# Seven half-size products for eight in a two-tile linear layer (one level of Strassen's algorithm)

## The chip, the cores and the metric

One core of one Trainium2 chip. The metric is the device time of one execution in microseconds (us). PE is TensorE's matmul stream, PEld its weight loads, DVE VectorE, ACT ScalarE, POOL GpSimd, SP the engine whose queue issues the DMAs.

## What is computed

```python
def _L0_cond_ref(x, weights, condition):
    W = weights[condition]
    return jnp.einsum('bct,bcd->bdt', x, W)

def _L0_ffn_ref(x, W, b, A, B, p_scores):
    C_CLAMP, EPS = 0.5, 1e-06
    z = jnp.einsum('bsd,od->bso', x, W) + b
    u = jnp.einsum('bsd,edr->ebsr', x, A)
    m = jnp.einsum('ebsr,ero,e->bso', u, B, p_scores)
    norm_z = jnp.linalg.norm(z, axis=-1, keepdims=True)
    norm_m = jnp.linalg.norm(m, axis=-1, keepdims=True)
    gamma = jnp.minimum(C_CLAMP * norm_z / (norm_m + EPS), 1.0)
    return z + gamma * m

x = x + _L0_ffn_ref(_L0_cond_ref(x, cond_weights, itok), W, b, A, B, p_scores)
```

x is 128 x 64 x 1024 in fp32, W is 1024 x 1024, the pair A, B has 8 x 16 = 128 inner columns, and each of the 128 batches picks one of 16 mixing matrices of 64 x 64.

## The kernel before

A tile is two batches: 128 rows of 1024. There are 64 tiles; four make a loop body (`step`, written out once before and once after the loop for the ends). For each tile PE does four things.

- `mix` (L419): eight fp32 matmuls give y transposed, in two halves of four chunks each, into `mix_ps`. ACT casts a half to `y_hi` (L245) and DVE makes the rest, `y_lo` (L333); both are fp32r, a form of fp32 that PE takes in one pass, and three matmuls (hi·hi, hi·lo, lo·hi) stand for one product.
- `linear` (L439): z in two halves of 512 columns, each 8 chunks x 3 passes = 24 matmuls with 512 columns.
- `down` (L430), once per two tiles: u, 24 matmuls of 256 columns. `up` (L456): m, six matmuls of 512 columns.

DVE adds the bias to each half (`add_bias`, L368), ACT squares and sums it (L289) and m (L313), POOL adds the residual to half 0 (L224) and takes the roots (L227, L232), DVE adds it to half 1, makes gamma (L388 to L401) and adds gamma·m (L408). SP loads x and stores the result. The mixers are copied by ACT from a table in SBUF (L253). Each engine has its own list of instructions; what orders them between engines are semaphores, written out by hand. In the head, ACT and DVE split W chunk by chunk (`split_w`, L241, L327), and the first tile's z takes each chunk as it comes:

```python
pe.wait_ge(w_hi_ready, k + 1)
pe.wait_ge(w_lo_ready, k + 1)
for h in range(2):
    summed = linear_chunk(0, h, k)
```

## Time and profile before

| | |
|---|---|
| three runs | 1031.59, 1031.59, 1031.82 us |
| profiled execution: span from first to last instruction | 1029.6 us |
| what lies around the span | about 2.0 us (run time less span) |
| instructions | 15207, of them 5260 matmul records |
| busy: PE, DVE, ACT, POOL | 1017.3, 351.2, 289.2, 165.2 us |
| mean granted clock of TensorE | 0.997 |
| moved by DMA | 73.58 MB |

Busy time is the time in which an engine had an instruction in it; matmuls are pipelined and overlap, so a group's sum can be above the span. The page also has the chain that ended last, the groups of instructions by line with what ended the idle time before them, and the DMA queues.

### The profile page before, as it was taken

How to read it: one execution, taken by the hardware profiler on the slowest of the kernel's cores; microseconds unless marked ns; L12 is line 12 of the kernel's file. 1: busy time of each engine (PE TensorE's matmuls, PEld its weight loads, DVE VectorE, ACT ScalarE, POOL GpSimd, SP SyncE). 2: the span in 40 equal slices, each digit the busy share in tenths (PEclk: the TensorE clock that was granted, in tenths of full speed). 3: DMA queues.
4: the chain of work that ended last, by engine and by line, in shares of the span. 5: the costliest groups of instructions: out<-in, count | busy, mean ns of one | idle time of the engine just before them, and what ended most of it. 6: DMA issues, size and time to landing. Idle time of an engine off the chain costs nothing.

```text
span 1029.6 us, 15207 instructions
## 1 busy us (share of the span) xinstructions
PE 1017.3 (99%) x5260; PEld 856.4 (83%) x5260; DVE 351.2 (34%) x620; ACT 289.2 (28%) x685; POOL 165.2 (16%) x263
## 2 busy tenths in 40 slices
...
PEclk9999999999999999999999999999999999999999
...
DMA packets 21367, 73.58 MB, mean 71 GB/s; under 512 B 2409, under 2 KB 3434, under 8 KB 21354
## 3 DMA queue, kind: packets, MB, share of 16 engines
...
q14 instruction: 5, 0.04, 0.0%
...
## 4 chain that ended last, share of the span: by engine, by line
PE 98%; DMA 1%; DVE 0%; ACT 0%; SPq 0%; issue 0%; DVEq 0%; POOLq 0%; POOL 0%; ACTq 0%
PE z_ps L439 70%; PE mix_ps L419 11%; PE m_ps L456 9%; PE u_ps L430 9%; DMA x_in<-in_x_dram 1%; DVE w_lo L327 0%; SPq L172 0%; ACT w_hi L241 0%; DVE rows L408 0%; DVE rows L368 0%; DVEq L59 0%; ACT squares L289 0%; POOLq L59 0%; ACT y_hi L245 0%; SPq L170 0%
## 5 line engine op out<-in xcount | busy, mean ns | idle before, releaser
L439 PE MATMUL z_ps<-w_hi,y_hi 128*128 128x512 f32 x1024 | 415.9, 406 | 2.2 <-DVE w_lo L327 2.2
L439 PE MATMUL z_ps<-w_hi,y_lo 128*128 128x512 f32 x1024 | 405.8, 396 | 0.0
L439 PE MATMUL z_ps<-w_lo,y_hi 128*128 128x512 f32 x1024 | 405.4, 396 | 0.0
L289 ACT ACTIVATE squares<-rows 128x512 bf16<-128x512 f32 x128 | 80.8, 631 | 628.2 <-DVE rows L368 536.8
L439 PEld LDWEIGHTS z_ps<-w_hi,y_lo 128*128 128x128 f32 x1024 | 192.7, 188 | 46.3
L439 PEld LDWEIGHTS z_ps<-w_hi,y_hi 128*128 128x128 f32 x1024 | 193.4, 189 | 43.0 <-ACT y_hi L245 2.4
L439 PEld LDWEIGHTS z_ps<-w_lo,y_hi 128*128 128x128 f32 x1024 | 193.4, 189 | 40.9
L368 DVE TENSOR_TENSOR rows<-z_ps,bias 128x512 f32<-128x512 f32 x128 | 88.6, 692 | 365.7 <-PE z_ps L439 365.7
L333 DVE TENSOR_TENSOR y_lo<-mix_ps,y_hi 128x512 fp32r<-128x512 f32 x128 | 88.2, 689 | 232.7 <-ACT y_hi L245 232.5
L224 POOL TENSOR_TENSOR rows<-rows,x_in 128x512 f32<-128x512 f32 x64 | 81.7, 1277 | 428.0 <-DVE rows L368 428.0
L419 PEld LDWEIGHTS mix_ps<-mixer,x_in 128*128 128x128 f32 x1024 | 131.3, 191 | 10.8 <-DMA x_in<-in_x_dram 2.3
L419 PE MATMUL mix_ps<-mixer,x_in 128*128 128x128 f32 x1024 | 134.6, 275 | 1.7 <-DMA x_in<-in_x_dram 1.7
L408 DVE SCALAR_TENSOR_TENSOR rows<-m_ps,gamma,rows 128x1024 f32<-128x1024 f32 (+1 forms) x65 | 82.3, 1268 | 2.2
L245 ACT CAST y_hi<-mix_ps 128x512 fp32r<-128x512 f32 x128 | 73.3, 572 | 18.3 <-PE mix_ps L419 18.3
L430 PE MATMUL u_ps<-y_hi,a_hi 128*128 128x256 f32 x256 | 71.8, 280 | 0.0
L430 PE MATMUL u_ps<-y_lo,a_hi 128*128 128x256 f32 x256 | 71.6, 280 | 0.0
L430 PE MATMUL u_ps<-y_hi,a_lo 128*128 128x256 f32 x256 | 71.4, 279 | 0.0
L313 ACT ACTIVATE squares<-m_ps 128x1024 bf16<-128x1024 f32 x64 | 65.5, 1023 | 2.3 <-PE m_ps L456 0.5
L229 POOL TENSOR_TENSOR z_sum<-z_sq 128x1 f32<-128x1 f32 x64 | 12.3, 193 | 315.4 <-ACT squares L289 315.4
L227 POOL TENSOR_TENSOR norm_m<-m_sq,half 128x1 f32<-128x1 f32 x64 | 35.1, 548 | 111.0 <-ACT squares L313 111.0
L430 PEld LDWEIGHTS u_ps<-y_lo,a_hi 128*128 128x128 f32 x256 | 48.2, 188 | 1.4
L430 PEld LDWEIGHTS u_ps<-y_hi,a_hi 128*128 128x128 f32 x256 | 48.1, 188 | 1.4
...
## 6 DMA issues: line engine op xcount, KB each, us to landing
x_in<-in_x_dram SPq DMA_DIRECT2D x64, 512.0 KB, 3.3
out_dram<-rows SPq DMA_DIRECT2D x63, 512.0 KB, 2.7
rows<-in_L_ffn_W_dram SPq DMA_DIRECT2D x4, 512.0 KB, 7.4
w_late<-in_L_ffn_W_dram SPq DMA_DIRECT2D x4, 512.0 KB, 11.0
...
a_in<-in_L_ffn_A_dram SPq DMA_DIRECT2D x1, 512.0 KB, 14.3
bm_in<-in_L_ffn_B_dram SPq DMA_DIRECT2D x1, 512.0 KB, 8.9
bias<-in_L_ffn_b_dram SPq DMA_DIRECT2D x1, 512.0 KB, 9.2
```

Source lines behind the costliest of these rows:

```text
L224: nc.gpsimd.tensor_tensor(result[:, j % 2, 0:H], z_b[:, j % 2, 0:H], x_in[:, j, 0:H], ALU.add).then_inc(residual_0_ready, 1)
L227: nc.gpsimd.tensor_tensor(norm_m[:, one], m_sq[:, one], half[:, :], ALU.pow).then_inc(norm_m_ready, 1)
L245: nc.scalar.copy(y_hi[:, j // 2 % 2, h * HC:(h + 1) * HC, j % 2 * P:(j % 2 + 1) * P], mix_ps[h][:, :].rearrange("p (k n) -> p k n", k=HC)) ...
L289: nc.scalar.activation(squares[:, cols], z_b[:, j % 2, cols], ACT.Square, accum_out=z_sq[:, j % 2, h:h + 1]).then_inc(z_squared, 1)
L313: nc.scalar.activation(squares[:, :], m_ps[:, :], ACT.Square, accum_out=m_sq[:, j % 2:j % 2 + 1]).then_inc(m_squared, 1)
L333: nc.vector.tensor_tensor(y_lo[part], mix_ps[h][:, :].rearrange("p (k n) -> p k n", k=HC), y_hi[part].bitcast(fp32), ALU.subtract).then_in ...
L368: nc.vector.tensor_tensor(z_b[:, j % 2, cols], z_ps[h][:, :], bias[:, cols], ALU.add).then_inc(z_b_ready, 1)
L408: nc.vector.scalar_tensor_tensor(out=result[:, j % 2, c], in0=m_ps[:, c], scalar=gamma[:, one], in1=result[:, j % 2, c], op0=ALU.mult, op1 ...
L419: mixed = nc.tensor.matmul(mix_ps[h][:, k * P:(k + 1) * P], x_in[:, j % BODY, (h * HC + k) * P:(h * HC + k + 1) * P], mixer[:, j % 2, :], ...
L430: summed = nc.tensor.matmul(u_ps[:, 0:2 * P], left[:, k, :], right[:, g, k, :], start=(k == 0 and n == 0), stop=(k == KC - 1 and n == 2))
L439: summed = nc.tensor.matmul(z_ps[h][:, :], left[:, g, k, r], right[:, k, h * H:(h + 1) * H], start=(k == 0 and n == 0), stop=(k == KC - 1 ...
L456: summed = nc.tensor.matmul(m_ps[:, c], left[:, r], right[:, c], start=(n == 0), stop=(n == 2))
```

## The change

Two tiles are a pair, and the pair's 256 rows are sorted anew into two row blocks of 128: block r holds 32 of the 64 output channels of each of the pair's four batches (the mixer's columns are laid out so that `mix` writes them in this order, 64 columns of either block per chunk and tile). With the two halves of the 1024 inner columns, Y is 2 x 2 blocks of 128 x 512, and W is 2 x 2 blocks of 512 x 512. In place of eight products come seven, in Winograd's form:

- S3 = Y11 − Y21, S2 = Y22 − S3, S4 = Y12 − S2, S1 = Y21 + Y22 on DVE, for each tile, read from PSUM; `y21` is a copy by ACT. S2 and S3 lie in `s23`, S4 and S1 are written back into `mix_ps`. All four are split into `s_hi` (ACT) and `s_lo` (DVE), as Y11, Y12, Y21, Y22 are into `y_hi`, `y_lo`.
- T1 = W12 − W11, T3 = W22 − W12, T2 = W22 − T1, T4 = W21 − T2 on POOL, once, in the head; the seven matrices W11, W21, W22, T1, T3, T4, T2 lie split in `w_hi`, `w_lo`. W is loaded in four chunks of a megabyte, through the two halves of `z` as staging space.
- P1 = Y11·W11 and P2 = Y12·W21 in bank `a_ps`; P6 = S2·T2, on top of it P7 = S3·T3, and later P4 = Y22·T4 in `b_ps`; P5 = S1·T1 and on top of it P3 = S4·W22 in `c_ps`. Each is 4 chunks x 3 passes = 12 matmuls of 512 columns (`product`).
- z11 = P1 + P2 + b, u2 = P1 + P6, u3 = u2 + P7, z12 = u2 + P5 + P3 + b, z21 = u3 + P4 + b, z22 = u3 + P5 + b: P1 is copied by ACT, the sums with a PSUM bank are DVE's, the bias for z12, z21 and z22 is added by POOL in SBUF.
- The residual is added by POOL for a whole row block (1024 columns), from `x_res`, which holds the x of one row block, loaded a second time in the new order of rows. The mixers are loaded by SP straight from DRAM, two small DMAs a tile, each behind a register load of the batch's id; their zeros are set once. x has two buffers in place of four. m's squares are taken in halves. `up` for pair p−1 stands within pair p, and for the last pair behind it.

```diff
+    W11, W21, W22, T1, T3, T4, T2 = range(7)
...
+w_hi = sb("w_hi", [P, 7, HC, H], fp32r)
+w_lo = sb("w_lo", [P, 7, HC, H], fp32r)
...
+y0_hi = sb("y0_hi", [P, HC, 2 * P], fp32r)
+y0_lo = sb("y0_lo", [P, HC, 2 * P], fp32r)
+y1_hi = sb("y1_hi", [P, 2, HC, 2 * P], fp32r)
+y1_lo = sb("y1_lo", [P, 2, HC, 2 * P], fp32r)
+s_hi = sb("s_hi", [P, 2, HC, 2 * P], fp32r)
+s_lo = sb("s_lo", [P, 2, HC, 2 * P], fp32r)
...
+mix_ps = pb("mix_ps", [P, 2, H])
+a_ps = pb("a_ps", [P, H])
+b_ps = pb("b_ps", [P, H])
+c_ps = pb("c_ps", [P, H])
...
+    for k in range(2, HC):
+        sp.wait_ge(w_lo_ready, 2 * (k - 1))
+        sp.wait_ge(t_lo_ready, 2 * (k - 1))
+        sp.dma_start(z[:, k % 2, :, :], w_steps[k]).then_inc(w_loaded[k], 16)
...
+    for k in range(HC):
+        st = z[:, k % 2, :, :]
+        pool.wait_ge(w_lo_ready, 2 * k + 1)
+        nc.gpsimd.tensor_tensor(st[:, 0, 0:H], st[:, 0, H:D], st[:, 0, 0:H], ALU.subtract).then_inc(t1_made, 1)
+        pool.wait_ge(w_lo_ready, 2 * k + 2)
+        nc.gpsimd.tensor_tensor(st[:, 0, H:D], st[:, 1, H:D], st[:, 0, H:D], ALU.subtract).then_inc(t13_made, 1)
+        pool.wait_ge(t1_made, k + 1)
+        pool.wait_ge(t13_made, k + 1)
+        nc.gpsimd.tensor_tensor(st[:, 1, H:D], st[:, 1, H:D], st[:, 0, 0:H], ALU.subtract).then_inc(t2_made, 1)
+        pool.wait_ge(t2_made, k + 1)
+        nc.gpsimd.tensor_tensor(st[:, 1, 0:H], st[:, 1, 0:H], st[:, 1, H:D], ALU.subtract).then_inc(t24_made, 1)
...
+        for j in range(2):
+            p = 2 * i + j
+            opening = first and j == 0
+            if not opening:
+                residual(p - 1, 1 - j, 0)
+                norm_z(p - 1, 1 - j, 0)
+                norm_m(p - 1, 0)
+                residual(p - 1, 1 - j, 1)
+                norm_z(p - 1, 1 - j, 1)
+            pool.wait_ge(u2_ready, p + 1)
+            nc.gpsimd.tensor_tensor(z[:, j, 0, H:D], z[:, j, 0, H:D], bias[:, H:D], ALU.add).then_inc(u2_biased, 1)
+            pool.wait_ge(u3_ready, p + 1)
+            nc.gpsimd.tensor_tensor(z[:, j, 1, H:D], z[:, j, 1, 0:H], bias[:, H:D], ALU.add).then_inc(u3_biased1, 1)
+            nc.gpsimd.tensor_tensor(z[:, j, 1, 0:H], z[:, j, 1, 0:H], bias[:, 0:H], ALU.add).then_inc(u3_biased0, 1)
+            if not opening:
+                norm_m(p - 1, 1)
...
+            if not opening:
+                split_s(2 * p + 1, 1, None)
+                act.wait_ge(z21_ready, p)
+                square_z(1 - j, 1, 0, 8 * p - 5)
+            act.wait_ge(p_done[1], p + 1)
             if opening:
...
+            nc.scalar.copy(z[:, j, 0, 0:H], a_ps[:, :]).then_inc(p1_ready, 1)
+            if not opening:
+                square_m(p - 1, 0)
+            if not opening:
+                square_m(p - 1, 1)
+            act.wait_ge(u_done, p + 1)
+            nc.scalar.copy(u_hi[:, :], u_ps[:, 0:2 * P]).then_inc(u_hi_ready, 1)
+            act.wait_ge(z22_ready, p + 1)
+            square_z(j, 1, 1, None if opening else 8 * p)
+            if not closing:
+                split_y(2 * p + 2, 0, 1 - j)
+            if not closing:
+                split_s(2 * p + 2, 0, p + 1)
+            act.wait_ge(z12_ready, p + 1)
+            square_z(j, 0, 1, 8 * p + 1)
+            act.wait_ge(z11_ready, p + 1)
+            square_z(j, 0, 0, 8 * p + 2)
+            if not closing:
+                split_y(2 * p + 3, 1, 1 - j)
...
+    def make_s(t):
+
+        dve.wait_ge(s3_made, t + 1)
+        nc.vector.tensor_tensor(s23[:, :, 0, :], block(1, 1), s23[:, :, 1, :], ALU.subtract).then_inc(s2_made, 1)
+        dve.wait_ge(s2_made, t + 1)
+        nc.vector.tensor_tensor(block(1, 0), block(1, 0), s23[:, :, 0, :], ALU.subtract).then_inc(s4_made, 1)
+        nc.vector.tensor_tensor(block(1, 1), block(1, 1), y21[:, :, :], ALU.add).then_inc(s1_made, 1)
+
+    def split_s(t, j):
+
+        for h in range(2):
+            dve.wait_ge(s_hi_ready, 2 * t + h + 1)
+            nc.vector.tensor_tensor(s_part(s_lo, j, h), s23[:, :, :, :] if h == 0 else mixed(1),
+                                    s_part(s_hi, j, h).bitcast(fp32), ALU.subtract).then_inc(s_lo_ready, 1)
...
+    split_y(0, 0, 0, True)
+    make_s(0)
+    split_w(0)
+    split_s(0, 0)
+    split_y(1, 1, 0)
+    split_w(1)
+    make_s(1)
+    split_t(0)
+    split_s(1, 1)
+    split_t(1)
+    for k in range(2, HC):
         split_w(k)
+        split_t(k)
...
+        for j in range(2):
+            p = 2 * i + j
+            opening, closing = first and j == 0, last and j == 1
+            if not opening:
+                make_s(2 * p + 1)
+                finish_z21(p - 1, 1 - j)
+                split_s(2 * p + 1, 1)
+                make_gamma(p - 1, 0)
+            dve.wait_ge(p_done[6], p + 1)
+            dve.wait_ge(p1_ready, p + 1)
+            nc.vector.tensor_tensor(z[:, j, 0, H:D], b_ps[:, :], z[:, j, 0, 0:H], ALU.add).then_inc(u2_ready, 1)
+            if not opening:
+                add_m(p - 1, 1 - j, 0)
+            dve.wait_ge(p_done[7], p + 1)
+            if not first:
+                dve.wait_ge(out_stored[1], 16 * (p - 1))
+            nc.vector.tensor_tensor(z[:, j, 1, 0:H], b_ps[:, :], z[:, j, 0, 0:H], ALU.add).then_inc(u3_ready, 1)
+            dve.wait_ge(p_done[5], p + 1)
+            dve.wait_ge(u3_biased1, p + 1)
+            nc.vector.tensor_tensor(z[:, j, 1, H:D], c_ps[:, :], z[:, j, 1, H:D], ALU.add).then_inc(z22_ready, 1)
+            dve.wait_ge(u_hi_ready, p + 1)
+            nc.vector.tensor_tensor(u_lo[:, :], u_ps[:, 0:2 * P], u_hi[:, :].bitcast(fp32),
+                                    ALU.subtract).then_inc(u_lo_ready, 1)
+            if not closing:
+                split_y(2 * p + 2, 0, 1 - j)
+                make_s(2 * p + 2)
+            dve.wait_ge(p_done[3], p + 1)
+            dve.wait_ge(u2_biased, p + 1)
+            nc.vector.tensor_tensor(z[:, j, 0, H:D], c_ps[:, :], z[:, j, 0, H:D], ALU.add).then_inc(z12_ready, 1)
+            if not closing:
+                split_s(2 * p + 2, 0)
+            if not opening:
+                make_gamma(p - 1, 1)
+                add_m(p - 1, 1 - j, 1)
+            dve.wait_ge(p_done[2], p + 1)
+            nc.vector.tensor_tensor(z[:, j, 0, 0:H], a_ps[:, :], bias[:, 0:H], ALU.add).then_inc(z11_ready, 1)
+            if not closing:
+                split_y(2 * p + 3, 1, 1 - j)
...
+    def product(bank, hi, lo, n, start):
+
+        for k in range(HC):
+            passes = [(hi, w_hi), (hi, w_lo), (lo, w_hi)]
+            for i, (left, right) in enumerate(passes):
+                summed = nc.tensor.matmul(bank[:, :], left[:, k, :], right[:, n, k, :],
+                                          start=(start and k == 0 and i == 0),
+                                          stop=(k == HC - 1 and i == 2), skip_group_check=not start)
...
-    def linear_chunk(j, h, k):
-
-        g, r = j // 2 % 2, slice(j % 2 * P, (j % 2 + 1) * P)
-        passes = [(y_hi, w_hi), (y_hi, w_lo), (y_lo, w_hi)]
-        for n, (left, right) in enumerate(passes):
-            summed = nc.tensor.matmul(z_ps[h][:, :], left[:, g, k, r], right[:, k, h * H:(h + 1) * H],
-                                      start=(k == 0 and n == 0), stop=(k == KC - 1 and n == 2))
-        return summed
-
-    def linear(j, h):
-
-        for k in range(KC):
-            summed = linear_chunk(j, h, k)
-        summed.then_inc(z_done, 1)
...
+            pe.wait_ge(y_lo_ready, 4 * p + 3)
+            if opening:
+                pe.wait_ge(w_hi_ready, 2 * (HC - 1) + 1)
+                pe.wait_ge(w_lo_ready, 2 * (HC - 1) + 1)
+            else:
+                pe.wait_ge(z11_ready, p)
+            product(a_ps, y0_hi[:, :, r0], y0_lo[:, :, r0], W11, True).then_inc(p_done[1], 1)
...
+                    pe.wait_ge(out_ready, 2 * p - 2)
+                up(0)
...
+            if opening:
+                pe.wait_ge(t_hi_ready, 2 * HC)
+                pe.wait_ge(t_lo_ready, 2 * HC)
+            else:
+                pe.wait_ge(z21_ready, p)
+            product(b_ps, s_hi[:, 0, :, r0], s_lo[:, 0, :, r0], T2, True).then_inc(p_done[6], 1)
+
+            pe.wait_ge(s_hi_ready, 4 * p + 4)
+            pe.wait_ge(s_lo_ready, 4 * p + 4)
+            if not opening:
+                pe.wait_ge(z12_ready, p)
+            product(c_ps, s_hi[:, 1, :, r1], s_lo[:, 1, :, r1], T1, True).then_inc(p_done[5], 1)
+
+            pe.wait_ge(u2_ready, p + 1)
+            product(b_ps, s_hi[:, 0, :, r1], s_lo[:, 0, :, r1], T3, False).then_inc(p_done[7], 1)
+
+            if not opening:
+                pe.wait_ge(out_ready, 2 * p - 1)
...
+            down(j)
+
+            if not closing:
+                pe.wait_ge(x_loaded[0], 16 * (p + 2))
+                pe.wait_ge(mixer_loaded[0], 16 * PER * (p + 2))
+                for h in range(2):
+                    mix(0, h)
+
+            pe.wait_ge(z22_ready, p + 1)
+            product(c_ps, s_hi[:, 1, :, r0], s_lo[:, 1, :, r0], W22, False).then_inc(p_done[3], 1)
+
+            pe.wait_ge(p1_ready, p + 1)
+            product(a_ps, y1_hi[:, j, :, r0], y1_lo[:, j, :, r0], W21, False).then_inc(p_done[2], 1)
+
+            if not closing:
+                pe.wait_ge(x_loaded[1], 16 * (p + 2))
+                pe.wait_ge(mixer_loaded[1], 16 * PER * (p + 2))
+                pe.wait_ge(s3_made, 2 * p + 3)
+                mix(1, 0)
+                pe.wait_ge(s_lo_ready, 4 * p + 6)
+                mix(1, 1)
+
+            pe.wait_ge(u3_ready, p + 1)
+            product(b_ps, y1_hi[:, j, :, r1], y1_lo[:, j, :, r1], T4, True).then_inc(p_done[4], 1)
...
     steps(pe, step)
+    pe.wait_ge(u_hi_ready, PAIRS)
+    pe.wait_ge(u_lo_ready, PAIRS)
+    for r in range(2):
+        pe.wait_ge(out_ready, 2 * PAIRS - 2 + r)
+        up(r)
```

**DVE, the middle of a pair.** Before, one tile in the written-out body (line numbers of the kernel before): y_lo for a later tile, the bias sums, gamma, the result.

```order
L333 TENSOR_TENSOR y_lo<-mix_ps,y_hi 128x4x128 [waits y_hi_ready]
L368 TENSOR_TENSOR rows<-z_ps,bias 128x512 [waits z_done]
L333 TENSOR_TENSOR y_lo<-mix_ps,y_hi 128x4x128 [waits y_hi_ready]
L388 TENSOR_SCALAR twice_m<-norm_m 128x1 [waits norm_m_ready]
L391 RECIPROCAL half_over_m<-twice_m 128x1 [waits twice_m_ready]
L368 TENSOR_TENSOR rows<-z_ps,bias 128x512 [waits z_done]
L396 TENSOR_TENSOR rows<-rows,x_in 128x512 [waits z_b_ready]
L401 TENSOR_SCALAR gamma<-norm_z,half_over_m 128x1 [waits over_m_ready,norm_z_ready]
L408 SCALAR_TENSOR_TENSOR rows<-m_ps,gamma,rows 128x1024 [waits residual_1_ready,residual_0_ready,gamma_ready]
```

With the change, from z12 (line numbers of the changed kernel; `s` is `s23`, `stats` holds the small columns): z12, the two s_lo of the next pair's first tile, gamma and the addition of m for block 1 of the pair before, z11, and y_lo, s3, y_lo of the next pair's second tile.

```order
L584 TENSOR_TENSOR z<-c_ps,z 128x512 [waits u2_biased,p3_done]
L504 TENSOR_TENSOR s_lo<-s,s_hi 128x8x64 [waits s_hi_ready]
L504 TENSOR_TENSOR s_lo<-mix_ps,s_hi 128x8x64 [waits s_hi_ready]
L511 TENSOR_SCALAR stats<-stats 128x1 [waits norm_m_ready]
L514 RECIPROCAL stats<-stats 128x1 [waits twice_m_ready]
L517 TENSOR_SCALAR stats<-stats 128x1 [waits over_m_ready,norm_z_ready]
L524 SCALAR_TENSOR_TENSOR z<-m_ps,stats,z 128x1024 [waits residual_ready,gamma_ready]
L591 TENSOR_TENSOR z<-a_ps,bias 128x512 [waits p2_done]
L485 TENSOR_TENSOR y_lo<-mix_ps,y_hi 128x8x64 [waits y21_ready,y_hi_ready]
L490 TENSOR_TENSOR s<-mix_ps,y 128x4x64 [waits s_lo_ready]
L485 TENSOR_TENSOR y_lo<-mix_ps,y_hi 128x8x64 [waits y_hi_ready]
```

The y_lo that the next pair's first product waits for now stands behind the addition of m and z11 on DVE, and z11 in its turn waits for P2.

**POOL, the head.** Before, the three memsets and then the first tile's work:

@@D2B
With the change the four sums of each of the four chunks of T stand there; these are those of chunk 0 and the first of chunk 1:

```order
L290 TENSOR_TENSOR z<-z 128x512 [waits w_lo_ready]
L292 TENSOR_TENSOR z<-z 128x512 [waits w_lo_ready]
L295 TENSOR_TENSOR z<-z 128x512 [waits t13_made,t1_made]
L297 TENSOR_TENSOR z<-z 128x512 [waits t2_made]
L290 TENSOR_TENSOR z<-z 128x512 [waits w_lo_ready]
```

Each waits for DVE's split of W (`w_lo_ready`) or for the sum before it.

**DVE, the head.** With the change, the splits of chunks 2 and 3 of W and T, in this order:

```order
L464 TENSOR_TENSOR w_lo<-z,w_hi 128x512 [waits w_hi_ready]
L467 TENSOR_TENSOR w_lo<-z,w_hi 128x2x512 [waits w_hi_ready]
L473 TENSOR_TENSOR w_lo<-z,w_hi 128x2x512 [waits t_hi_ready]
L476 TENSOR_TENSOR w_lo<-z,w_hi 128x2x512 [waits t_hi_ready]
L464 TENSOR_TENSOR w_lo<-z,w_hi 128x512 [waits w_hi_ready]
L467 TENSOR_TENSOR w_lo<-z,w_hi 128x2x512 [waits w_hi_ready]
L473 TENSOR_TENSOR w_lo<-z,w_hi 128x2x512 [waits t_hi_ready]
L476 TENSOR_TENSOR w_lo<-z,w_hi 128x2x512 [waits t_hi_ready]
```

Chunk 3 of W (L464, L467, the second time) stands behind the split of chunk 2's T, which waits for ACT's casts of what POOL has made.

## Rows read from the trace of the kernel before

**Rows 1.** The page, busy time and the span in 40 slices (PEclk, tenths of full speed):
```profile
PE 1017.3 (99%) x5260; PEld 856.4 (83%) x5260; DVE 351.2 (34%) x620; ACT 289.2 (28%) x685; POOL 165.2 (16%) x263
...
PEclk9999999999999999999999999999999999999999
```

**Rows 2.** The page, the chain that ended last, shares of the span:
```profile
PE z_ps L439 70%; PE mix_ps L419 11%; PE m_ps L456 9%; PE u_ps L430 9%; DMA x_in<-in_x_dram 1%; DVE w_lo L327 0%; SPq L172 0%; ACT w_hi L241 0%; DVE rows L408 0%; DVE rows L368 0%; DVEq L59 0%; ACT squares L289 0%; POOLq L59 0%; ACT y_hi L245 0%; SPq L170 0%
```

**Rows 3.** That chain in order of time (start us, us, what):
```profile
507.88 5.60 PE z_ps L439 x24
...
539.43 5.60 PE z_ps L439 x24
```

**Rows 4.** Timeline of PE (start us, us): first `up` and `down`, and what follows each:
```profile
513.32 0.63 PE L456 MATMUL m_ps<-b_hi,u_hi 128*128 128x512 f32 x2
...
514.72 1.05 PE L419 MATMUL mix_ps<-mixer,x_in 128*128 128x128 f32 x8
...
521.22 0.28 PE L430 MATMUL u_ps<-y_hi,a_hi 128*128 128x256 f32 x1
...
524.02 1.05 PE L419 MATMUL mix_ps<-mixer,x_in 128*128 128x128 f32 x8
```

**Rows 5.** Timeline of the end (start us, us):
```profile
1022.28 0.40 PE L439 MATMUL z_ps<-w_hi,y_lo 128*128 128x512 f32 x1
...
1024.51 0.55 POOL L232 TENSOR_TENSOR norm_z<-z_sum,half 128x1 f32<-128x1 f32 x1
...
1025.34 1.41 DVE L408 SCALAR_TENSOR_TENSOR rows<-m_ps,gamma,rows 128x512 f32<-128x512 f32 x2
1026.12 0.99 SPq L202 DMA_DIRECT2D out_dram<-rows  x2
```

**Rows 6.** The page, DMA issues (count, KB each, median us to landing):
```profile
x_in<-in_x_dram SPq DMA_DIRECT2D x64, 512.0 KB, 3.3
rows<-in_L_ffn_W_dram SPq DMA_DIRECT2D x4, 512.0 KB, 7.4
```

**Rows 7.** Timeline around 500 us, handoffs between engines (start us, us):
```profile
502.97 0.57 ACT L245 CAST y_hi<-mix_ps 128x512 fp32r<-128x512 f32 x1
...
503.57 0.69 DVE L333 TENSOR_TENSOR y_lo<-mix_ps,y_hi 128x512 fp32r<-128x512 f32 x1 [3.57 <-ACT y_hi L245]
...
504.17 0.14 DVE L388 TENSOR_SCALAR twice_m<-norm_m 128x1 f32<-128x1 f32 x1
...
506.60 0.40 PE L439 MATMUL z_ps<-w_hi,y_lo 128*128 128x512 f32 x1
...
507.12 0.69 DVE L368 TENSOR_TENSOR rows<-z_ps,bias 128x512 f32<-128x512 f32 x1 [2.60 <-PE z_ps L439]
```

**Rows 8.** Groups by line (line engine op, count | busy us, mean ns | idle before):
```profile
L368 DVE TENSOR_TENSOR rows<-z_ps,bias 128x512 f32<-128x512 f32 x128 | 88.6, 692 | 365.7 <-PE z_ps L439 365.7
L333 DVE TENSOR_TENSOR y_lo<-mix_ps,y_hi 128x512 fp32r<-128x512 f32 x128 | 88.2, 689 | 232.7 <-ACT y_hi L245 232.5
L224 POOL TENSOR_TENSOR rows<-rows,x_in 128x512 f32<-128x512 f32 x64 | 81.7, 1277 | 428.0 <-DVE rows L368 428.0
L408 DVE SCALAR_TENSOR_TENSOR rows<-m_ps,gamma,rows 128x1024 f32<-128x1024 f32 x63 | 80.9, 1284 | 2.2
L289 ACT ACTIVATE squares<-rows 128x512 bf16<-128x512 f32 x128 | 80.8, 631 | 628.2 <-DVE rows L368 536.8 <-issue 91.4
L245 ACT CAST y_hi<-mix_ps 128x512 fp32r<-128x512 f32 x128 | 73.3, 572 | 18.3 <-PE mix_ps L419 18.3
L377 DVE TENSOR_TENSOR u_lo<-u_ps,u_hi 128x256 fp32r<-128x256 f32 x32 | 13.3, 416 | 1.1 <-ACT u_hi L299 1.1
L327 DVE TENSOR_TENSOR w_lo<-w_late,w_hi 128x1024 fp32r<-128x1024 f32 x4 | 4.9, 1224 | 1.1 <-ACT w_hi L241 1.0
L241 ACT CAST w_hi<-w_late 128x1024 fp32r<-128x1024 f32 x4 | 4.2, 1050 | 1.5 <-DMA w_late<-in_L_ffn_W_dram 1.5
```

**Rows 9.** View of windows, the head (us, PE, PEld, DVE, ACT, POOL busy, PEclk, DMA, GB/s):
```profile
12.50:16.00 3.50, 3.50 (x10) 2.71 (x10) 3.50 (x4) 3.14 (x4) 0.00 (x0) 0.54 1.03 412
```

More of the change, by code:

```diff
@@ L107, in conditioned_clamped_low_rank_linear_kernel @@
-        z_b = rows[:, 0:2, :]
-        result = rows[:, 2:4, :]
-        w_in = [rows[:, k, :] if k < 4 else w_late[:, k - 4, :] for k in range(KC)]
-        mix_ps = [pb(f"mix_ps{h}", [P, H]) for h in range(2)]
-        z_ps = [pb(f"z_ps{h}", [P, H]) for h in range(2)]
+        y21 = sb("y21", [P, HC, C], fp32)
+        s23 = sb("s23", [P, HC, 2, C], fp32)
+        z = sb("z", [P, 2, 2, D], fp32)
+        squares = sb("squares", [P, H], bf16)
+        cond_ids = sb("cond_ids", [1, B], i32)
+        stats = sb("stats", [P, 40], fp32)
@@ new lines, in conditioned_clamped_low_rank_linear_kernel, with z_sq, stat @@
+        half = stats[:, 0:1]
+        p_col = stats[:, 1:2]
+        table_out = stats[:, 2:3]
+        def z_sq(par, r, h):
+            return stats[:, 4 + 4 * par + 2 * r + h:5 + 4 * par + 2 * r + h]
+        def stat(n, r):
+            return stats[:, 12 + 2 * n + r:13 + 2 * n + r]
+        Z_SUM, NORM_Z, M_SQ0, M_SQ1, M_SUM, NORM_M, TWICE_M, HALF_OVER_M, GAMMA = range(9)
+        idle = squares[:, :]
+        a_in = x_res[:, :].rearrange("p (k n) -> p k n", k=KC)
+        bm_in = z[:, 1, 1, :]
```

587 lines of the change are left out of this document (291 added, 296 removed).

## The prediction, made before the changed kernel was run

> **What bounds the kernel now.** The page first: PE is busy 99% of 1029.6 us, at a granted clock of nine tenths or more in every slice [rows 1]. Busy time alone proves little, since matmuls overlap; the chain that ended last does: 98% of it is PE, 70% the z products [rows 2]. So every matmul removed counts in full, as long as the others stay behind PE. The chain in order of time gives the rates. The same piece of 24 z matmuls (one half of one tile) recurs after 31.55 us, which is two tiles, and takes 5.60 us, 0.2333 us a matmul [rows 3]. The 0.40 us in the groups is latency, not rate. In the timeline of PE the six matmuls of `up` take 514.72 − 513.32 = 1.40 us and the 24 of `down` 2.80 us [rows 4]. Two tiles are thus 96 z matmuls (22.40), two `up` (2.80), one `down` (2.80) and, as the rest, 3.55 for the mixes. 32 pairs of tiles are 1009.6 us; 20.0 us of the span are head and tail. From the last matmul's start, 0.23 us before its nominal end, to the end are 7.3 us, so the tail is 7.1 and the head loses 12.9 [rows 5]. The three runs stand at 1031.59 to 1031.82, 2.0 us above the profiled span; I add 2.0 to every span.
>
> **The products.** Seven products of 12 matmuls replace 96 per pair: 12 fewer, in the same shapes (512 columns against a 128x128 weight). Over 32 pairs: 384 x 0.2333 = **−89.6 us**. `up`, `down` and the mixes keep their counts and sizes. A pair is then 28.76 us of PE. SP's queue gets, per pair, four small mixer loads, each behind a register load, and two loads of residual rows into one buffer, on top of its two x loads and two stores. On the scale of the walk below a residual load is asked for at 1.2, when POOL has used the rows before, lands 3.3 us later [rows 6] at about 5 and is wanted at 6.9; the next is asked for at 9.5 and wanted at 26.8. The x and mixer loads asked for at 18.6 and 26.0 are wanted a whole pair later. SP's waits stand in the order in which they are met (1.2, 9.4, 9.4, 18.6, 25.3, 26.0). So they cost nothing; without that cover the first residual load would be 1.9 us of slack gone, on POOL.
>
> **Is PE still covered within a pair?** I walk one pair from the start of P1 (product P1 = 0). PE: P1 to 2.8, `up` 4.2, P6 7.0, P5 9.8, P7 12.6, `up` 14.0, `down` 16.8, mix of the next pair's first tile 18.6, P3 21.4, P2 24.2, mix of its second tile 26.0, P4 28.8. The handoffs: PE to DVE 0.29 us after a product's nominal end (last matmul 506.60 + 0.23, DVE at 507.12), ACT to DVE 0.03, DVE to its next queued operation 0.09 before the first has ended (503.57 + 0.69, next at 504.17) [rows 7]. Durations are those of [rows 8]: 0.69 for 512 columns on DVE (0.60 in a queue), 0.42 for 256 (0.33), 0.57 for an ACT cast (0.37 taken for 256 columns), 0.63 for a square, 1.05 and 1.22 for 1024 columns on ACT and DVE, 1.28 for a POOL sum.
> The tightest chain starts at the end of `down`. ACT: u_hi at 17.1, the square of z22, y_hi, the copy y21 to 18.9. DVE in its new order: y_lo, s3, y_lo, s2, s4 (behind its own semaphore), s1 to 21.6; z12 (P3 plus 0.29 is 21.7) to 22.3; two s_lo to 23.5; three small operations of gamma and the 1024-column addition of m to 25.3; z11 to 26.0. ACT: square 26.7, y_hi and y21 27.5; DVE y_lo 28.2. PE wants that y_lo for the next P1 at 28.8: 0.4 us to spare. Behind it DVE makes s2, s4, s1, then z21 and s_lo by 31.6; P6 wants it at 28.8 + 4.2 = 33.0: 1.4 to spare. The mix at 24.2 wants the s_lo of 23.5 and only for its second half, at 25.1. P7 wants u2 (ready at 8.1) at 9.8. The second `up` wants the first half's m to be consumed at 12.6: `up` ends 4.2, four squares of which two come first to 6.0, POOL's sum and root to 6.9, gamma, u2, addition 9.4. P3 wants z22 at 18.6: P7 12.6, u3 13.6, one POOL sum 14.9, z22 15.6. POOL does two residuals of 1024 columns (at most 2.6 each), three bias sums and eight small operations, some 12 us of 28.8; ACT about 11, DVE about 16. All is covered, the tightest point by 0.4. If queued operations did not overlap, a dozen of them would come 0.09 later each and the y_lo at about 29.2: a wait of 0.45 in each of 31 pairs, 14 us. I take zero, as the row of queued DVE operations shows the overlap, and keep 14 for the range.
>
> **The head.** Before, the first tile's z followed the weights chunk by chunk. Now P6, the second product, waits for all of T, each block of which passes ACT, DVE, POOL, ACT, DVE. One chunk from its landing: two ACT casts 1.5, DVE's 1.22, POOL's T3, T2, T4 at 1.28 plus 0.08 each, 4.1, ACT 1.1, DVE 1.3: 9.3 us. Only two chunks fit in the staging space; the third is asked for when the first is wholly done. I walk it: first weights at 10.4 (SP has issued the id, x and first mixer loads by about 5.8, and a megabyte takes the 4.6 worked out below); DVE makes tile 0's y_lo and sums to 11.5, splits chunk 0 by 13.3 and s by 14.5; only then may the second half of tile 1's mix go, so ACT casts its y_hi by 16.3, and both engines work through chunk 1 and T of chunk 0 until 22.6. SP asks for chunk 2. Its megabyte lands 4.6 us later: the 3.3 of half a megabyte [rows 6] plus 1.3 for the other half at some 400 GB/s, the rate of the stretch when the weights came [rows 9]; the upper bound is the 7.4 of a crowded queue [rows 6]. 27.2 + 9.3 = 36.5. Chunk 3 has landed by then, but ACT and DVE take it only after T of chunk 2; it is done at about 45.5. PE has by then done the pair's mixes (3.55) and P1 (2.80): it has lost 39.1. Its clock had fallen after an idle stretch: from 12.5 to 16.0 it was granted 0.54, the lower of its two levels (1.2 and 2.4 GHz) most of that time, and started 10 matmuls in 3.5 us, where 15 fit [rows 9]: 1.2 us, which P6 pays again, and some more for a longer idle stretch, say 1.6. P7 waits about 0.5 for u2, as DVE is held by b_lo, whose load waits for the last T. Head 41.2 (39.1 + 1.6 + 0.5) against 12.9: **+28.3 us**.
> Now POOL's sums read SBUF beside DVE's subtractions of two SBUF operands. No row shows the two at once: POOL's 1.28 us was measured alone. Bounds: nothing, or each waits for the other's whole instruction; on the path that is T1 before DVE's second split (1.0) and DVE's T1/T3 split before T4 (1.2), 2.2 a chunk over three chunks, 6.6 us. I take 3.1, near the middle. The Trainium skill, "SBUF — State Buffer", section "Who interferes with whom", speaks against the change here: a DVE instruction with two SBUF inputs and a GpSimd instruction that reads SBUF exclude each other, and the second waits until the first is through. By that the term would be the upper bound.
>
> **The tail.** Both `up`s of the last pair come after P4, one behind the other, since m has one buffer. From P4's end: `up` 1.4, two squares to 3.3, POOL sum and root (0.55 [rows 5]) 4.1, gamma 4.8, addition 6.0, `up` 7.6, squares 9.4, POOL 10.3, gamma 10.9, addition 12.2, and the store as before (2.9 from the end of the last addition, 1026.75, to the span's end [rows 5]) with a little for twice the size: 15.4. Of it 2.8 is work already counted: 12.6 against 7.1, **+5.5 us**.
>
> **Sum.** 1029.6 − 89.6 + 28.3 + 5.5 + 3.1 = 976.9; plus 2.0: **979 us**.
>
> **Rivals.**
> (a) The chain of DVE and ACT sets the pair. For it: only 0.4 us to spare, eleven large DVE operations in a row. Against: the overlap in [rows 7]. Price 14 us: 993.
> (b) POOL and DVE exclude each other fully in the head, the rule named above: 6.6 in place of 3.1, 982.5. In the pairs it changes nothing: the one subtraction of two SBUF operands per tile stands at 22.3 and about 31, where POOL has no large sum (its residual runs from 26.8 to 29.4).
> (c) Slower than before. The new operations read and write runs of 64 columns, and some write back into PSUM. If each of the 13 such operations in the tight chain took 0.25 us more, the pair would be 3.25 − 0.4 = 2.85 longer, 31 x 2.85 = 88: 1067. It is slower from (1029.6 + 2 − 976.9) / 31 + 0.4 = 2.2 us a pair, 0.17 an operation. Against: y_lo, written in runs of 128, takes 0.689, and the whole-row addition 0.692 [rows 8].
> (d) The saving isn't there: 979 + 89.6 = 1069. The order of instructions has 84 product matmuls a pair, so only a lower granted clock or slower matmuls could take it back; the clock stood at nine tenths or more under the same load [rows 1].
>
> **Chances.** Forecast 0.57, (a) 0.22, (b) 0.15, (c) 0.04, (d) 0.02. Low end: no meeting of POOL and DVE (−3.1) and a head 4 us shorter by my walk: 972. High end: (a) with (b), 996.5, and a late chunk 2 in part: 998. A measurement of this kernel tells about 0.2% (2 us) from no change. Faster by more 0.93, the same 0.01, slower 0.06.
>
> **What would show it.** PE about 4876 matmuls; a pair 28.8 us from P1 to P1, with no wait for y_lo, z11 or s_lo beyond tenths; P6 of the first pair at 45 to 51 us and PE idle before it; in the head POOL's sums at 1.28 us if nothing interferes, longer, or DVE's splits longer than 1.22, if something does; the last P4 15.4 us before the end. Wrong: a pair of 29.2 or more with PE waiting for y_lo (rival a), DVE operations of 64-column runs well above 0.69 (c).

## The result, and the profile after

The changed kernel takes 1101.76 us (median of 4 runs, 1100.42 to 1102.92) against 1031.59 (4 runs, 1030.78 to 1031.82): ratio 1.0681, 95% interval 1.0666 to 1.0696. It is slower by 70 us where I forecast faster by 53, and it lies far outside my range.

The page of the kernel after: busy time, PEclk, the queue, the chain that ended last by engine and by line, three groups, two DMA issues.

```profile
span 1100.4 us, 15748 instructions
...
PE 959.1 (87%) x4876; PEld 813.0 (74%) x4876; DVE 521.8 (47%) x1011; ACT 382.8 (35%) x916; POOL 389.6 (35%) x439
...
PEclk7599999999999999999999999999999999999995
...
q1 hardware_dynamic: 47098, 108.54, 30.7%
...
DMA 25%; PE 25%; POOL 16%; DVE 13%; SPq 9%; issue 7%; ACT 3%; ACTq 0%; DVEq 0%; POOLq 0%
...
L617 PE MATMUL c_ps<-w_hi,s_hi 128*128 128x512 f32 x256 | 115.0, 449 | 72.6 <-DVE z L575 72.6
...
L575 DVE TENSOR_TENSOR z<-c_ps,z 128x512 f32<-128x512 f32 x32 | 22.1, 692 | 208.4 <-POOL z L334 208.4
...
x_in<-in_x_dram SPq DMA_DIRECT2D x64, 512.0 KB, 9.8
```

Three things against [rows 1, 2, 6]. The 384 matmuls are gone (5260 to 4876 records), but PE is busy 87% of the span, not 99%. The chain, which was 98% PE, is a quarter DMA and a quarter PE. And an x load that landed in 3.3 us now takes 9.8, although the queue's packets fill less than a third of the 16 engines' time: a slow transfer on idle engines.

The waits of the kernel after (engine, line, waited for: us in total, times, longest) name the links. The matmuls into c_ps wait for z22 (L575), z22 waits for POOL's bias sum (L334), and that sum stands in POOL's queue behind a residual (L305) that waits for its load:

```profile
DVE z L575 <- POOL z L334: 208.4, 32, 7.1
POOL z L305 <- DMA x_res<-in_x_dram: 178.0, 24, 9.0
...
PE c_ps L617 <- DVE z L575: 72.6, 30, 2.7
```

One pair, from P1 at 526.42. First the chain that ended last, in order of time (start us, us, what), then SP's timeline of the same stretch, then POOL's:

```profile
528.93 11.69 DMA x_res<-in_x_dram
...
540.68 2.39 POOL z L305
...
543.82 1.27 POOL z L332
545.09 1.23 POOL z L334
546.41 0.70 DVE z L575
```

```profile
523.30 0.69 SPq L267 DMA_DIRECT2D out_dram<-z  x1
524.27 0.36 SPq L270 DMA_DIRECT2D x_in<-in_x_dram  x1
525.87 2.77 SPq L219 DMA_DIRECT2D mixer<-in_L_cond_weights_dram  x2
528.93 0.71 SPq L256 DMA_DIRECT2D x_res<-in_x_dram  x1
```

```profile
524.74 2.41 POOL L305 TENSOR_TENSOR z<-z,x_res 128x1024 f32<-128x1024 f32 x1 [8.88 <-ACT squares L391]
...
540.68 2.39 POOL L305 TENSOR_TENSOR z<-z,x_res 128x1024 f32<-128x1024 f32 x1 [7.59 <-DMA x_res<-in_x_dram]
```

On the scale of my walk (P1 = 0): POOL is through with the rows of block 0 at 0.7 (forecast 1.2). SP asks for block 1's rows at 2.5, since a store, an x load and two mixer loads stood ahead; the data are used at 14.3 (forecast 6.9). Behind that residual come two bias sums (L332, L334), and z22 is done at 20.7 (forecast 15.6); P3 starts right behind it, at 547.16 (forecast 18.6 on the scale of the walk). The view of windows shows how the load spends its 11.7 us; its columns are us, then PE, PEld, DVE, ACT, POOL busy, PEclk, DMA share, GB/s:

```profile
533.00:535.00 2.00, 2.00 (x10) 1.69 (x9) 1.74 (x5) 0.00 (x0) 0.09 (x1) 1.00 0.25 99
535.00:537.00 2.00, 2.00 (x10) 1.65 (x9) 0.65 (x1) 0.00 (x0) 0.00 (x0) 1.00 0.26 105
```

A quarter of the DMA engines' time, about 100 GB/s: what four of 16 engines would give. Over the whole 11.69 us the view gives 97 GB/s at a share of 0.26. That is 1.1 MB, twice the load's half megabyte, so something else moved beside it; e6, below, says what. Before, an x load (asked for at 508.84, landed at 512.08, the first row) and a store (asked for at 511.20, the second row), both with 128 rows outermost, ran like this (same columns; between 510.5 and 511.0 the load had 377 GB/s at a share of 1.00):

```profile
510.00:511.00 1.00, 1.00 (x6) 0.78 (x6) 1.00 (x2) 0.00 (x0) 0.00 (x0) 1.00 0.80 279
...
512.00:513.00 1.00, 1.00 (x6) 0.82 (x5) 0.00 (x0) 0.00 (x0) 0.00 (x0) 1.00 0.97 393
```

The stall can cost more than its length. In the pair before this one PE stood still for 2.6 us, from the end of the mixes (started 510.10) to P3 at 514.69; soon afterwards the granted clock fell to 0.50, the lower level, and the twelve matmuls of P3 started over 4.1 us instead of the 2.6 of e5, below. P3 is as slow as that, 3.6 to 4.2 us, in 19 of the 30 pairs between the first and the last. The view of windows (same columns):

```profile
516.00:518.00 2.00, 2.00 (x7) 1.54 (x6) 1.83 (x4) 0.63 (x2) 0.00 (x0) 0.50 0.36 99
```

**Where the 123.5 us between my forecast span and the profiled one lie** (1100.4 − 976.9). Second P1 at 78.30, by my walk 73.8 (44.3 lost in the head, 3.55 for the first mixes, and 28.76 less the two `up`s, 2.80, that the first pair lacks): +4.5. Thirty pairs from there to P1 at 1043.53 are 32.17 us each against 28.76: +102.4. Last P1 to the end of the last P4, 27.4 against 25.2 (84 product matmuls 19.6, two `up`s, `down`): +2.2. From there to the end, 29.5 against 15.4: +14.1. Together 123.2; the rest is rounding.

### The profile page after: what moved, and what is told of

The parts are those of the page before. It is cut to its first block, busy times and chain, and to the rows that moved or that the text cites. A ratio compares the mean times of both kernels' runs of the same rounds, so it can differ in the third digit from the quotient of the medians.

```text
span 1100.4 us, 15748 instructions
## 1 busy us (share of the span) xinstructions
PE 959.1 (87%) x4876; PEld 813.0 (74%) x4876; DVE 521.8 (47%) x1011; ACT 382.8 (35%) x916; POOL 389.6 (35%) x439
## 4 chain that ended last, share of the span: by engine, by line
DMA 25%; PE 25%; POOL 16%; DVE 13%; SPq 9%; issue 7%; ACT 3%; ACTq 0%; DVEq 0%; POOLq 0%
DMA x_res<-in_x_dram 24%; PE c_ps L617 11%; POOL z L305 7%; PE b_ps L617 6%; PE a_ps L617 4%; SPq L219 4%; POOL z L332 3%; POOL z L334 3%; SPq L217 3%; DVE s_lo L504 2%; DVE z L524 2%; PE m_ps L640 2%; DVE z L575 2%; DVE z L584 1%; PE mix_ps L607 1%
## 5 line engine op out<-in xcount | busy, mean ns | idle before, releaser
L305 POOL TENSOR_TENSOR z<-z,x_res 128x1024 f32<-128x1024 f32 x64 | 153.4, 2397 | 514.9 <-ACT squares L391 273.5
L617 PE MATMUL c_ps<-w_hi,s_hi 128*128 128x512 f32 x256 | 115.0, 449 | 72.6 <-DVE z L575 72.6
L617 PE MATMUL a_ps<-w_hi,y_hi 128*128 128x512 f32 x256 | 103.4, 404 | 32.1 <-DVE w_lo L464 25.5
L575 DVE TENSOR_TENSOR z<-c_ps,z 128x512 f32<-128x512 f32 x32 | 22.1, 692 | 208.4 <-POOL z L334 208.4
L617 PE MATMUL c_ps<-w_lo,s_hi 128*128 128x512 f32 x256 | 110.9, 433 | 0.0
L617 PE MATMUL c_ps<-w_hi,s_lo 128*128 128x512 f32 x256 | 110.5, 432 | 0.0
L617 PE MATMUL b_ps<-w_hi,s_hi 128*128 128x512 f32 x256 | 100.7, 393 | 4.3 <-DVE w_lo L476 4.3
L617 PE MATMUL a_ps<-w_lo,y_hi 128*128 128x512 f32 x256 | 101.7, 397 | 0.0
L617 PE MATMUL a_ps<-w_hi,y_lo 128*128 128x512 f32 x256 | 100.6, 393 | 0.0
L617 PE MATMUL b_ps<-w_lo,s_hi 128*128 128x512 f32 x256 | 100.5, 393 | 0.0
L617 PE MATMUL b_ps<-w_hi,s_lo 128*128 128x512 f32 x256 | 100.5, 393 | 0.0
L572 DVE TENSOR_TENSOR z<-b_ps,z 128x512 f32<-128x512 f32 x32 | 22.1, 692 | 106.7 <-PE b_ps L617 106.7
```

The costliest lines, as they stand in the source:

```text
L305: nc.gpsimd.tensor_tensor(z[:, par, r, :], z[:, par, r, :], x_res[:, :], ALU.add).then_inc(residual_ready, 1)
L575: nc.vector.tensor_tensor(z[:, j, 1, H:D], c_ps[:, :], z[:, j, 1, H:D], ALU.add).then_inc(z22_ready, 1)
L617: summed = nc.tensor.matmul(bank[:, :], left[:, k, :], right[:, n, k, :], start=(start and k == 0 and i == 0), stop=(k == HC - 1 and i == ...
```

## The experiments

Theory T, after seeing the trace: `x_rows` and `out_rows` put 4 blocks of 32 rows outermost on the DRAM side, such a transfer runs on four DMA engines, the residual load is late, and the bias sums that P3 needs are queued behind it on POOL. The Trainium skill, "DMA: Bandwidth & Descriptors", section "Why a DMA increments its semaphore by 16 and not by 1", has the rule: a DMA is spread over the largest number up to 16 that divides the outermost sizes of both its sides, and takes the lowest-numbered engines. By it 128 partitions against 4 blocks give four engines. The shares of 0.25 and 0.26 above agree.

The result, e9 and e10 are timed several times; every other run is one execution. The kernel before, run beside them, took 1029.7 to 1033.7 us, so that differences of up to 4 us between chips say nothing.

**e1, the transfers in four pieces.** Each load and store becomes four DMAs of 32 rows:

```diff
-sp.dma_start(x_res[:, :], x_rows[p, 0])
+for b in range(2 * PER):
+    sp.dma_start(x_res[b * CH:(b + 1) * CH, :], x_rows[p, 0, b])
```

> Theory T (transfers): a residual load or a store whose DRAM side is 4 blocks of 32 rows moves at a quarter of the rate (98 GB/s, DMA share 0.26, against 0.9 to 1.0 and about 400 GB/s in the kernel before), so the load lands 11.7 us after its issue and POOL starts the residual, and with it the bias sums behind it, late. Here each of these transfers is four, one per block of 32 whole rows, same bytes. T expects a landing of 4 to 5 us, PE's wait for z22 gone, the pair 32.2 to about 29 us, the time at about 1000 us. Rival Q (the queue of SP): what is late is the issue, since SP's list stands behind mixer loads and stores; 12 more issues a pair at 0.4 to 0.6 us make it worse: pair at or above 32.2, 1100 us or more.

Measured 969.51 us (before, same chip, 1033.65). Pairs are 28.27 us throughout and the chain is 93% PE again. The page, DMA issues and the residual's group:

```profile
L315 POOL TENSOR_TENSOR z<-z,x_res 128x1024 f32<-128x1024 f32 x64 | 154.0, 2407 | 327.8 <-ACT squares L401 315.4
...
x_in<-in_x_dram SPq DMA_DIRECT2D x64, 512.0 KB, 3.3
x_res<-in_x_dram SPq DMA_DIRECT2D x256, 128.0 KB, 2.5
```

With only the form of the transfers changed, all of the loss is gone and 64 us of gain appear. That is 30 us below the 1000 I had expected here, since nothing at all was left of the loss in the pairs.

**e3, only POOL's order.** The transfers stay slow; the residual and norm of block 1 move behind the bias sums:

```diff
 norm_m(p - 1, 0)
-residual(p - 1, 1 - j, 1)
-norm_z(p - 1, 1 - j, 1)
 ...
 nc.gpsimd.tensor_tensor(z[:, j, 1, 0:H], z[:, j, 1, 0:H], bias[:, 0:H], ...)
+residual(p - 1, 1 - j, 1)
+norm_z(p - 1, 1 - j, 1)
 norm_m(p - 1, 1)
```

> Only POOL's list is changed: the residual and norm of block 1 of the pair before go behind the three bias sums. The transfers stay as slow. Theory T expects PE's wait for z22 (2.3 us a pair) to go, as the bias sums no longer stand behind a late load; the late residual then holds DVE's addition of m and with it z11, so a part comes back at P1: pair 30 to 31.5 us, 1035 to 1080 us. If the load's lateness did not matter, only the order, the pair is 29 us and the time about 1010.

Measured 983.71 us. Pairs are 28.3 here too (28.27 in most, 28.60 at most), though POOL waits for the load longer than in the changed kernel, and more often:

```profile
POOL z L305 <- DMA x_res<-in_x_dram: 259.7, 31, 9.8
POOL z L332 <- DVE z L572: 124.8, 32, 4.2
```

The second row is the bias sum that z22 needs; it now waits for its own input, u3 (L572), alone. So the slow load harms the pairs only through what stands behind it on POOL. That is stronger than I had expected: I had thought the late residual would still be felt. What is left against the clean layout (e5, below) is the end: its last two loads and its last store are on the path, and from the end of the last P4 to the end e3 takes 30.5 us against 17.6.

**e4, SP's queue.** The mixer loads are left out of the steady pairs (later tiles are computed with the mixers of the first ones, so their outputs are others; PE does the same work).

```diff
 sp.dma_start(x_in[:, 0, :], x_tiles[2 * p + 4])
-load_mixer(2 * p + 4, 0)
```

> The two mixer loads of each pair's tiles are left out after the first four tiles (later tiles are mixed with the matrices of tiles 2 and 3), so SP is free of four register loads and four DMA issues a pair, some 8 us of its time, and DMA of 128-byte packets. Theory T: the load of block 1 is issued at most 2 us earlier and lands as slowly: pair 31 to 32, time 1060 to 1095. Rival Q: pair 29, time about 1000.

Measured 1088.13 us, pairs at 31.7. The mixers ahead of the load on SP are worth some 14 us of 1101.8, half a microsecond a pair, and are not the cause.

**e5, another layout.** Row block r takes batch r of both tiles instead of half of each batch, so that a load or store is two DMAs of 64 consecutive rows and the mixer keeps its natural order of columns:

```diff
-x_rows = x.rearrange("(n b) (r d) t -> n r b d t", b=2 * PER, r=2)
+x_rows = x.rearrange("(n j r) c t -> n r j c t", j=2, r=PER)
```

> Row block r is batch r of both tiles (2 runs of 64 rows) in place of half the channels of all four batches (4 runs of 32); the mixer's layout is then the natural one, one run of 256 bytes a row. Residual loads and stores are two transfers of 64 rows each. Theory T: as with four transfers, landing 4 to 5 us, pair about 28.9 us, time 990 to 1000; a little under the four-transfer kernel because SP issues six DMAs fewer a pair. Rival Q: between 1070 and 1100.

Measured 968.83 us, pairs 28.27: again well below what I had expected (990 to 1000), as in e1.

**e2 and e6, loads or stores alone in four pieces.** Each has one half of e1's edit.

> The residual loads alone are split into four DMAs of 32 rows; the stores keep the form of the change. Theory T (the bias sums stand behind the residual on POOL, and the residual waits for a load that takes 10 us): pairs at 28.3 us as with both split, and only the end is later, because the last store keeps its 10.5 us where the split one takes about 4: 969.5 + 6 = 976 us. Rival S (the stores, as slow and as many, hold up the x loads or the loads that are in flight with them): pairs between 28.3 and 32.2, 990 to 1080 us.

> The stores alone are split into four DMAs of 32 rows; the loads keep the form of the change. Theory T: the load still takes 9 to 12 us, POOL and then PE still wait, pairs at 31 to 32.2 us, end 6 us sooner than the change: 1060 to 1096 us. Rival S: pairs near 28.3 to 29, 975 to 995 us.

Measured: e2 978.77, e6 998.99 (before, same chip, 1031.16). Both parts matter, and neither theory had e6. With the loads split, pairs are 28.27 and the slow stores cost nearly only the end: 9 us in all, 8.4 of them behind the last product. With the stores split and the loads slow, pairs are 29.14 us on average, not the 31 to 32.2 that I expected and not 28.3 either. The chain of e6 in order of time, and a window with its load alone (columns as above):

```profile
519.65 8.22 DMA x_res<-in_x_dram
...
527.94 2.39 POOL z L315
```

```profile
523.00:525.00 2.00, 2.00 (x11) 1.65 (x10) 1.66 (x5) 0.00 (x0) 0.17 (x1) 1.00 0.25 96
```

Its load takes 8.3 us instead of 11.7, though it runs at the same quarter share. In the changed kernel a store of half a megabyte in the slow form, asked for at 523.30, shares that quarter with the load behind it: 1.1 MB moved between the load's issue and its use. So slow stores lengthen the slow loads. Of the 3.9 us a pair (32.17 − 28.27), slow loads alone make 0.9 (e6), slow stores alone nothing (e2), and the other 3.0 come only where both are slow.

**e8, fewer engines.** Each load and store becomes two DMAs of two blocks:

```diff
-sp.dma_start(x_res[:, :], x_rows[p, r])
+for j in range(2):
+    sp.dma_start(x_res[j * C:(j + 1) * C, :], x_rows[p, r, PER * j:PER * (j + 1)])
```

> Loads and stores each as two DMAs of 2 blocks x 32 rows x 1024. Theory N (a DMA is spread over as many engines as its outermost blocks allow: 4 blocks went on 4 of 16, share 0.26 at 98 GB/s): 2 blocks go on 2 engines each. If the two DMAs take the same two, a load moves at some 50 GB/s, 12 to 20 us instead of 9 to 12, and pairs are well above 32.2, 35 to 40 us: 1190 to 1340 us. If they take different ones, it is 4 engines again: pairs 31.5 to 32.5, 1080 to 1110 us. Rival O (what counts is the number of DMAs in flight or their size, or that the rows are strided in DRAM): two DMAs of half the size come near the time of two DMAs of 64 rows, 969 to 985 us.

Measured 1431.58 us, pairs 41.8 and 43.5 in turn. The chain in order of time, and a window within the second load (columns as above):

```profile
693.10 16.78 DMA x_res<-in_x_dram
709.95 2.40 POOL z L317
...
713.35 19.09 DMA x_res<-in_x_dram
732.51 2.35 POOL z L317
```

```profile
725.00:727.00 2.00, 2.00 (x20) 2.00 (x19) 0.00 (x0) 0.37 (x1) 0.00 (x0) 1.00 0.13 53
```

Half the share (0.13), half the rate (53 GB/s), with as many DMAs and bytes as e5, which is at 968.8: what counts is the size of the outermost dimension. The two DMAs of a load went on the same two engines, since a second pair of engines would show a share of 0.25. So did the stores: in the 19.09 us of the load a store was pending as well, and the share stayed at 0.13, for 52 GB/s or 1.0 MB, twice the load. Both parts of the rule from the Trainium skill's page above stand. Pairs went above my 35 to 40 because load, residual, load, residual now follow each other through the one buffer `x_res` (16.8, 2.4, 19.1 and 2.4 us above). The x loads suffer too (16.1 us to landing), but PE never waits for one in the pairs.

**e7 and e11, the head.** In the changed kernel, POOL's T sums and DVE's splits stretch each other (timelines of the kernel after, POOL and then DVE; the second DVE row stands beside no POOL sum):

```profile
24.61 2.28 DVE L476 TENSOR_TENSOR w_lo<-z,w_hi 128x1024 fp32r<-128x1024 f32 x1
...
29.08 1.21 DVE L473 TENSOR_TENSOR w_lo<-z,w_hi 128x1024 fp32r<-128x1024 f32 x1
```

```profile
22.34 1.27 POOL L292 TENSOR_TENSOR z<-z 128x512 f32<-128x512 f32 x1 [1.16 <-DVE w_lo L467]
23.75 2.06 POOL L295 TENSOR_TENSOR z<-z 128x512 f32<-128x512 f32 x1
25.89 2.12 POOL L297 TENSOR_TENSOR z<-z 128x512 f32<-128x512 f32 x1
```

e7 is e5 with the sixteen sums on DVE:

```diff
-nc.gpsimd.tensor_tensor(st[:, 0, 0:H], st[:, 0, H:D], st[:, 0, 0:H], ALU.subtract)
+nc.vector.tensor_tensor(st[:, 0, 0:H], st[:, 0, H:D], st[:, 0, 0:H], ALU.subtract)
```

> Kernel e5 (two batches a row block, 968.8 us) with the sixteen T sums of the head moved from POOL to DVE. Theory X (POOL and DVE shut each other out in the head: sums of 1.27 us took up to 2.2, splits of 1.22 up to 2.3): every sum takes 0.6 to 0.7 us, the splits stay at 1.22, and P6 of the first pair starts near 41 to 44 instead of 52: 968.8 - 9 = 960 us, range 957 to 963. Rival Y (the head is set by the landings and by ACT's casts, so that the meeting costs nothing): P6 stays at 50 to 53, 967 to 970 us. Rival Z (DVE has too much to do in the head, with 2.7 us of sums a block in its own queue): P6 later than 52, above 970 us.

Measured 960.23 us; P6 of the first pair at 43.49 instead of 52.26, every sum 0.68 to 0.69 us and every 1024-column split 1.21 to 1.23. But DVE's sums are also twice as fast, so e11 puts sixteen idle sums back on POOL beside them:

```diff
+seen = w_hi[:, W11, k, :].bitcast(fp32)
+nc.gpsimd.tensor_tensor(squares[:, :], seen, seen, ALU.subtract)
```

> The kernel of e9 (T sums on DVE, 960.7 us, P6 of the first pair at 43.5) plus sixteen sums on POOL that nothing uses, 512 columns each, two SBUF operands, released by the same semaphores as POOL's T sums were; the output is the same. Nobody waits for POOL in that stretch but through DVE. Theory X (a POOL sum and a DVE operation of two SBUF operands shut each other out): DVE's T sums and splits last 0.7 to 1.2 us longer wherever POOL stands beside them, POOL's sums 0.7 to 1.2 us longer too, P6 starts 8 to 16 us later, at 51 to 60, and the kernel takes 968 to 977 us. Rival Y (in e7 only DVE's faster sums counted, the meeting was free): durations and P6 as in e9, 960 to 962 us.

Measured 970.88 us (before, same chip, 1029.69); P6 at 54.18, 10.7 us later than in e9, and the kernel 10.2 us slower, for work that nobody waits for. DVE's rows, groups by line of the first 60 us, in e9 and then in e11 (four sums of each line):

```profile
L470 DVE TENSOR_TENSOR z<-z 128x512 f32<-128x512 f32 x4 | 2.8, 692 | 0.1
...
L465 DVE TENSOR_TENSOR z<-z 128x512 f32<-128x512 f32 x4 | 2.7, 681 | 0.0
```

```profile
L473 DVE TENSOR_TENSOR z<-z 128x512 f32<-128x512 f32 x4 | 5.2, 1311 | 0.0
...
L478 DVE TENSOR_TENSOR z<-z 128x512 f32<-128x512 f32 x4 | 4.2, 1052 | 0.1
```

```profile
L303 POOL TENSOR_TENSOR squares<-w_hi 128x512 bf16<-128x512 f32 x16 | 24.8, 1549 | 24.8 <-DVE w_lo L483 23.1
```

The meeting is real and on the path. It is not wholly one after the other, though. In the last block of e11, from the start of POOL's first sum at 44.86 to the end of DVE's fourth at 51.70, 6.8 us, POOL does four sums and DVE four sums and most of a split: about 5.1 and 3.8 us if each were alone, 8.9 together.

**e9 and e10, timed.**

> The kernel of e7 again, timed for an interval: two batches a row block, T sums on DVE. One execution gave 960.23 against 1031.16. If that stands: 959.5 to 961 us, ratio to the kernel before 0.930 to 0.932. If it was a favourable execution: up to 965.

> The kernel of e5 again, timed for an interval: two batches a row block, T sums on POOL as in the change. One execution gave 968.83. If that stands: 968 to 970 us, ratio 0.938 to 0.941, and 8.5 us behind e9, all of it ahead of the second product of the first pair.

e9 (the kernel of e7): 960.70 us (960.18 to 961.36, 5 runs) against 1031.28 (9 runs), ratio 0.9317, interval 0.9304 to 0.9330. e10 (the kernel of e5): 969.84 (968.97 to 970.50, 4 runs), ratio 0.9401, interval 0.9387 to 0.9416. The difference, 9.1 us, is that of P6's start (52.76 in e10, 43.52 in e9).

## Why the prediction was wrong, point by point

- **The step that failed: "a residual load is asked for at 1.2 … lands 3.3 us later [rows 6] at about 5 and is wanted at 6.9 … So they cost nothing".** It landed 11.7 us after its issue, asked for at 2.5, and held POOL to 14.3. I took the 3.3 us from the x load of the kernel before, a transfer of the same size but of 128 rows outermost, for one whose DRAM side has 4 blocks outermost. The size was the same, the form was not, and the rate went from 377 GB/s to about 100. e1, e5 and e8 settle this. The diff's `x_rows` line showed the form, so it could have been read before.
- **The price put on lost cover: "the first residual load would be 1.9 us of slack gone, on POOL".** This named POOL, but not what is queued behind the residual there. Two bias sums and through them z22 and P3 came late. e3 shows that this place in the queue, not the lateness by itself, makes the pairs slow.
- **SP's queue.** The load was asked for 1.8 us after the rows were free, behind an x load and two mixer loads; I had put it at once. e4 leaves the mixers out: 0.5 us a pair.
- **The stores.** I gave them no term in the pairs. They are as slow as the loads, and on the same engines. With the loads slow they make 3.0 of the 3.9 us a pair (e6 against the changed kernel), with the loads mended nothing (e2).
- **The pair.** Right once the transfers are mended: forecast 28.76, measured 28.27 (e1, e2, e3, e5, e9). Most of the half microsecond is the matmul: in the products of e5 the starts are 0.227 to 0.233 us apart by bank, where [rows 3] gave 0.2333, and the 84 of them take 19.27 instead of 19.60. The mixes take 3.41 instead of 3.55, the two `up`s 2.72 instead of 2.80, `down` 2.87 instead of 2.80.
- **Rival (a), the chain of DVE and ACT,** did not come: the point with 0.4 us to spare held in every kernel with clean transfers, with no wait of PE in its pairs.
- **Rival (c), runs of 64 columns:** y_lo takes 0.687 us in the kernel after, 0.689 before. No cost at all. My rivals on the slower side, (c) and (d), gave 1067 and 1069, the right direction for reasons that were wrong; (c)'s threshold of 2.2 us a pair also set a span against a run time (2.1 is right).
- **Rival (d):** the records fell by 384, and the granted clock did fall after stalls (PEclk 0.50 above), but as a consequence. The 24 matmuls a pair into c_ps start 0.272 us apart on average over the 30 pairs, against 0.2325 in e5: 0.9 us of the 3.9. PE's wait for z22 is 2.4 more (72.6 over 30), and its wait for the next pair's y_hi ahead of P1 0.2. The last 0.4 is not placed.
- **The head.** P6 at 52.8 in the changed kernel; 45.5 + 3.1 forecast, 52.1 with rival (b)'s 6.6. These 4.2 us are nearly all of the 4.5 by which the second P1 came late. POOL's sums met by DVE took 2.06 to 2.19 us (one 1.71) instead of 1.27, the 1024-column splits up to 2.28 instead of 1.21. Rival (b) had the size, and I had given it 0.15, although the Trainium skill's "SBUF — State Buffer", section "Who interferes with whom", spoke for it; the rows of the kernel after come near to it (5.65 us of work took 5.2, from 23.30 to 28.5, where full exclusion would need 5.65), those of e11 agree only in part (8.9 us of work took 6.8, as above).
- **The tail.** 15.4 forecast, 29.5 in the changed kernel, 17.6 in e5. Of the 14.1 too many, 11.9 go with the slow last load (asked for at 1072.36, used at 1083.99) and the slow last store (10.5 us from the last addition to the end, against 2.9 before [rows 5]). The other 2.2 remain in e5, whose last store takes 4.2 and whose second `up` ran at the lower clock.
- **The sum with the mended step.** Forecast span 976.9; e5 measured 967.0. Its head and pairs differ by +2.9 and −14.8, its last pair by −0.5 and its tail by +2.2, on my own division (73.8, 28.76, 25.2, 15.4): −10.2 together, against −9.9.

Not settled: why the matmuls of the products start a little closer together than before. I made no run for it. That slow stores lengthen the slow loads is read from e2 and e6 and from the bytes moved beside one load; the trace does not name the engine of a packet. And why POOL's sums and DVE's operations overlap in part in e11 was not tried apart.
